# Attention on one core: prob x val in bursts of four key chunks, and the row maxima dealt anew over the units of a slot

## What is computed

```python
x = x + _L0_conv_ref(_gn(x), Wq, bq, Wk, bk, Wv, bv)     # layer 0
    q = q.reshape(B * NUM_HEADS, S, hd)                  # k and v alike; S = 1024, hd = 64
    scores = jnp.einsum('gqd,gkd->gqk', q, k) / sqrt(hd)
    attn = jax.nn.softmax(scores, axis=-1)
    wv = jnp.einsum('gqk,gkd->gqd', attn, v)             # "prob x val"
x = x + _L1_conv_ref(_gn(x), ...)                        # layer 1: masked relu, 3x3 convolution
```

## Time and profile before

| | us |
|---|---|
| median of 3 runs (2612.68 to 2613.2) | 2612.98 |
| the profiled execution | 2614.79 |
| its span in the trace | 2613.0 |
| PE busy in it | 2527.8 (97%) |
| DVE busy | 1942.0 (74%) |
| POOL busy | 1139.0 (44%) |
| ACT busy | 1089.0 (42%) |

### The profile page before, as it was taken

One profiled execution on the slowest core, in us unless ns is written; L12 is line 12 of the kernel. 1 busy time (PEld: TensorE's weight loads), 2 busy tenths in 40 slices (PEclk: granted clock), 3 DMA queues, 4 the chain that ended last, 5 costly groups with the idle time before them and its releaser, 6 DMA issues.

```text
span 2613.0 us, 39802 instructions
## 1 busy us (share of the span) xinstructions
PE 2527.8 (97%) x11848; PEld 994.2 (38%) x11848; DVE 1942.0 (74%) x2646; ACT 1089.0 (42%) x1803; POOL 1139.0 (44%) x971
## 2 busy tenths in 40 slices
PE   6999999999999999999999999988999999999998
PEld 2333333333333333333333333332344444444443
DVE  5877787787788787777778888886576967967415
ACT  4455455455545545545554554446232132132100
POOL 1465476566557646655664765545103012030000
PEclk9999999999999999999999999999999999999999
DMA  5324243251533415333242442511443734633533
GB/s 157 83 71 117 67 128 87 60 136 50 127 82 97 111 36 142 91 79 105 71 120 73 117 105 57 132 49 61 161 170 131 271 130 161 239 132 129 199 117 151
DMA packets 209638, 300.63 MB, mean 115 GB/s; under 512 B 82192, under 2 KB 131472, under 8 KB 209424
## 3 DMA queue, kind: packets, MB, share of 16 engines
q1 hardware_dynamic: 209424, 297.97, 38.3%
HBM read 194.49 MB, written 52.69 MB: 95 GB/s over the span
## 4 chain that ended last, share of the span: by engine, by line
PE 83%; DVE 9%; issue 3%; DMA 2%; ACT 1%; SPq 1%; POOL 1%; DVEq 0%; ACTq 0%; POOLq 0%
PE bank L844 27%; PE bank L747 15%; PE bank L721 14%; PE bank L676 11%; PE bank L694 7%; PE bank L686 6%; DVE nmax L1261 2%; DVE prob_sum L1255 2%; PE bank L710 1%; ACT prob L927 1%; PE bank L702 1%; PE bank L734 1%; DVE bn L221 1%; DVE qk_lo L1247 1%; SPq L414 1%
## 5 line engine op out<-in xcount | busy, mean ns | idle before, releaser
L1261 DVE TENSOR_REDUCE nmax<-bank 128x1 f32<-128x512 f32 x1024 | 658.2, 682 | 222.9 <-PE bank L694 215.6
L927 ACT ACTIVATE prob<-bank 128x512 f32<-128x512 f32 x1024 | 555.9, 595 | 589.3 <-PE bank L721 573.2
L844 PE MATMUL bank<-v,u_slab 128*128 128x512 f16 x3456 | 748.6, 380 | 0.0
L1090 POOL TENSOR_TENSOR prob_sum<-prob_sum,prob 128x512 f32<-128x512 f32 x354 | 513.3, 1450 | 371.7 <-ACT prob L927 370.6
L747 PE MATMUL bank<-prob,val 128*64 128x512 f32 x2048 | 497.5, 607 | 0.0
L844 PEld LDWEIGHTS bank<-v,u_slab 128*128 128x128 f16 x3456 | 338.5, 98 | 408.2 <-issue 3.0
L694 PE MATMUL bank<-k_a,q_a 128*128 128x512 f16 x1024 | 384.6, 382 | 18.3 <-DVE nmax L1261 12.3
L1255 DVE TENSOR_TENSOR prob_sum<-prob_sum,prob 128x512 f32<-128x512 f32 x354 | 356.5, 1007 | 11.4 <-DVE shift L1271 8.9
L721 PE MATMUL bank<-q_a,k_a 128*128 128x512 f16 x1024 | 315.2, 381 | 17.0 <-ACT prob L927 16.1
L721 PE MATMUL bank<-q_b,k_b 128*128 128x512 f16 x1024 | 305.2, 380 | 1.4 <-DMA q_b<-shift 1.1
L747 PEld LDWEIGHTS bank<-prob,val 128*64 128x64 f32 x2048 | 124.6, 136 | 238.3 <-issue 192.9
(11 more groups left out here) (139 smaller groups left out, 2503.6 us busy)
## 6 DMA issues: line engine op xcount, KB each, us to landing
u_slab<-u_scratch SPq DMA_DIRECT2D x72, 1024.0 KB, 5.0
xs<-x SPq DMA_DIRECT2D x28, 1024.0 KB, 5.5
tile<-x_scratch SPq DMA_DIRECT2D x26, 1024.0 KB, 6.2
u_scratch<-u_w SPq DMA_DIRECT2D x96, 192.0 KB, 2.7
q_a<-qk_hi SPq DMA_DIRECT2D x64, 256.0 KB, 4.8
den_sb<-recip_scratch SPq DMA_DIRECT2D x128, 128.0 KB, 2.9
x_scratch<-xr SPq DMA_DIRECT2D x16, 1024.0 KB, 4.4
xr<-x SPq DMA_DIRECT2D x15, 1024.0 KB, 7.6
```

Of the source, the lines that this page charges most:

```text
L844: mm = pe.matmul(bank_at(pos, co)[:].rearrange("p (i n) -> p i n", i=2), slab[:, l, c, co * P:(co + 1) * P], image[v][:, 2 * c:2 * c + 2, ...
L927: act.activation(prob[:, (2 * u + e) % 8], sc_bank[bank_turn(s * 16 + 2 * u + e, 16 * HPI)[0]][:], ACT.Exp, scale=float(D) ** -0.5).then_i ...
L1090: nc.gpsimd.tensor_tensor(acc, in0, prob[:, (2 * kc + 1) % 8], ALU.add).then_inc(s1["sum1"], 1)
L1261: dve.tensor_reduce(nmax[:, m // 2, m % 2:m % 2 + 1], src[:], AX.X, ALU.max, negate=True)\
```

## The change

In slots with projections (`has_projections`) the probabilities are multiplied in bursts of four key chunks: chunks 0 to 3 at the end of unit 4 and 4 to 7 at the end of unit 0 of the next slot; where s % 4 = 2 the second four stay in two pairs, 4,5 in unit 6 and 6,7 in the next unit 0. Other slots keep their four pairs. In the same slots the maxima are dealt 3, 3, 1, 3, 3, 3 over units 0 to 5. No instruction is added or removed; they stand in another order. Of `exp_tile` and its waits nothing is changed.

```diff
+MAX_QUOTA_FOURS = [3, 3, 1, 3, 3, 3, 0, 0]
...
-def ring_items(u, nxt, prev, v_units, stat):
+def ring_items(u, nxt, prev, v_units, stat, quota):
...
+def has_projections(s, more):
+
+    return s % HPH < 3 and (s < HPH or more)
...
+def max_quota(s, more):
+
+    return MAX_QUOTA_FOURS if has_projections(s, more) else MAX_QUOTA
...
+def pv_burst(s, u, more):
+
+    if not has_projections(s, more):
+        at = {2: (0, 1), 4: (2, 3), 6: (4, 5), UNITS: (6, 7)}
+    elif s % HPH == 2:
+        at = {4: (0, 1, 2, 3), 6: (4, 5), UNITS: (6, 7)}
+    else:
+        at = {4: (0, 1, 2, 3), UNITS: (4, 5, 6, 7)}
+    return at.get(u, ())
...
                     if u == 0 and prev:
-                        weigh_pair(h - 1, (s - 1) % HPI, SEG // 2 - 1, den_direct(s - 1, more))
-                    if u >= 2 and u % 2 == 0:
-                        weigh_pair(h, s, u // 2 - 1, den_direct(s, more))
+                        weigh_burst(h - 1, (s - 1) % HPI, pv_burst((s - 1) % HPI, UNITS, more), den_direct(s - 1, more))
+                    weigh_burst(h, s, pv_burst(s, u, more), den_direct(s, more))
```

More of the change, by code:

```diff
@@ L98, in bank_turn @@
     return bank_of(n), next(d for d in range(1, period) if bank_of(n - d) == bank_of(n))
-def ring_items(u, nxt, prev, v_units, stat):
-    first = sum(MAX_QUOTA[:u])
-    tiles = [("max", first + k) for k in range(MAX_QUOTA[u])] if nxt else []
+def ring_items(u, nxt, prev, v_units, stat, quota):
+    first = sum(quota[:u])
+    tiles = [("max", first + k) for k in range(quota[u])] if nxt else []
     at = {"a": tiles[0:1], "b": tiles[1:2], "c": tiles[2:]}
@@ L749, in weigh, with weigh_burst @@
                               stop=(kc == SEG - 1)).then_inc(s1["pv_done"], 1)
-            def weigh_pair(h, s, n, direct=False):
-                for kc in (2 * n, 2 * n + 1) if direct else ():
+            def weigh_burst(h, s, chunks, direct=False):
+                for kc in chunks if direct else ():
                     sum_prob(h, kc)
-                for kc in (2 * n, 2 * n + 1):
+                for kc in chunks:
                     weigh(h, s, kc)
@@ L764, in slot @@
                     items = ring_items(u, nxt, "direct" if den_direct(s - 1, more) else prev, proj and r == 2,
-                                       stat_units(s, more))
+                                       stat_units(s, more), max_quota(s, more))
                     def run(place):
@@ L828, in _ @@
                 slot(B - 1, s, nxt=s < HPI - 1, more=False)
-            weigh_pair(B * HPI - 1, HPI - 1, SEG // 2 - 1, True)
+            weigh_burst(B * HPI - 1, HPI - 1, pv_burst(HPI - 1, UNITS, False), True)
             def group_sum(pair, k):
```

## The result

| | before | after |
|---|---|---|
| median, us | 2612.83 (4 runs, 2611.42 to 2613.20) | 2626.91 (4 runs, 2624.99 to 2633.04) |
| profiled execution | 2614.79 | 2624.99 |
| its span | 2613.0 | 2623.2 |

The ratio is 1.0054, with a 95% interval of 1.0041 to 1.0067: the changed kernel is slower by half a per cent. Between the medians lie 14.1 us, between the spans of the two profiled executions 10.2. The forecast was 2622.3, and 2624.1 for the profiled execution, 9.3 us more than before.

A forecast was written before the change was run, and what follows sets the result against it. PE's own instruction order was taken to bound the slots. Bursts -11.3, ACT +12.9, DVE +5.5, slots 2 and 6 +0.7 and edges +1.5 made +9.3 on 2612.98: 2622.3 us, range 2609 to 2641 (own case 2618.5 to 2629).

The forecast's parts named there:

- Check (6): Profile sign: a full image of the loop grows by 1.2 us.
- The bursts, -11.3: Slots with projections: 75 bursts of probability matmuls fewer, each saving PE 0.15 us; -11.3 us.
- ACT, +12.9: Slots 0, 1, 4, 5: unit 6 too short for ACT, so unit 7's second matmul waits 0.51 us (slot 1: 0.24).
- Check (1): Profile sign: PE's wait for exponentials rises 8 to 10 us, some 22 idle times of 0.35 in unit 7.
- check 5: Profile sign: from unit 2 to unit 3 PE does not wait for ACT.
- DVE, +5.5: Slots 0 and 1: unit 2 too short for DVE with moments; unit 3's third maximum waits 0.42 us, 13 times.
- check 3: Profile sign: unit 3's third maximum waits for DVE by 0.4 us in slots 0 and 1, not 4 and 5.
- Slots 2 and 6, +0.7: New unit 3 waits of 1.05 us replace old ones of 1.0: net +0.05 in 14 slots.
- check (4): Profile sign, slots 2 and 6: unit 3's third maximum waits 0.5 us, the value projection 0.55.
- The rival of the port: Slots 2 and 6: POOL's adding starts before DVE's and takes the port; +18 us, 2640 us; 20%.
- Edges, +1.5: Very first slot about +1 us, last image between -1 and +2; +1.5 us taken for both, an estimate.
- The savings alone: Rival: PE stays unbroken and only the saved bursts show, 2601.7 us; 10%.

The follow-up runs named there:

- experiment 10: Kernel before, with only one burst of four in unit 4 of slots 4 and 5, replacing the pairs of units 2 and 4, old maxima; 2609.76 us, 0.9986.
- Experiment 3: Changed kernel, but slots 0, 1, 4 and 5 keep a pair of chunks 4,5 in unit 6, with 6,7 in the next unit 0; 2621.45 us, 1.0033.
- experiment 4: Changed kernel, but ACT evacuates unit 5's last projection behind the first exponential of unit 6, not ahead of it; 2632.79 us, 1.0074.
- Experiment 6: Changed kernel, but in unit 2 of slots 0 and 1 DVE copies the sums ahead of the two moments; 2623.47 us, 1.0034.
- experiment 2: Kernel before with only the maxima dealt 3,3,1,3,3,3 in slots with projections, all bursts as before; 2611.29 us, 0.9989.
- experiment 8: Kernel before with only the maxima of slots 2 and 6 dealt 3,3,2,3,3,2; 2617.58 us, 1.0016.
- Experiment 5: Changed kernel, but the very first slot has the old maxima and pairs of chunks in units 2 and 4; 2620.44 us, 1.0024.
- experiment 9: Changed kernel undone but for the burst of four in unit 4 of slots 4 and 5 and the new maxima, old first slot; 2607.58 us, 0.9980.
- experiment 7: Changed kernel with pair 4,5 in unit 6 of slots 0, 1, 4, 5; slots 2 and 6 rearranged; sums first; old first slot; 2613.33 us, 0.9998.
- experiment 1: Changed kernel's bursts with the maxima dealt as before, 2,3,3,3,3,2; 2652.42 us, 1.0155.

## Why the prediction was right, step by step

**The bound.** PE's order is the time in the slots; DVE's busy share fell to 72% instead of rising. Check (6), a full image, measured +1.4 for +1.2. The medians moved by 14.1 us for the 9.3 forecast, and the interval of the ratio, 10.7 to 17.5 us, leaves 9.3 just out; the spans of the profiled executions moved by 10.2.

**The bursts, -11.3.** Right. 3.59 us for four chunks (check 2), 0.15 a burst, and experiment 10 shows it alone.

**ACT, +12.9.** Right in mechanism, place and size: 0.52 for 0.51 in slots 0, 4, 5 and 0.28 for 0.24 in slot 1. Check (1) asked for some 22 equal idle times; 21 are there, of the 0.35 foretold, and the 22nd, slot 1 of the last image, has none. The sum of the list rose by 7.0 us and not by 8 to 10, since older waits for ACT went. Experiment 3 takes the waits away with a pair of chunks as cover, and in experiment 4 ACT's work has no room in the other order either. The case that the same order makes a wait from unit 2 to unit 3 was excluded by 0.17 us of slack, and none is there (check 5): unit 2 lasts 1.75 and unit 3 4.10 in slots 4 and 5.

**DVE, +5.5.** The mechanism is right (check 3: slots 0 and 1, not 4 and 5), and the size was 0.30 for 0.42: I had let the bank be freed 0.2 us behind the end of the copy, and it took 0.11. So 13 x 0.30 = 3.9. Experiment 6 removes it from unit 3. What I did not ask was who else takes a ring bank behind the moments: the statistics' matmul in unit 4 of slot 1, 7 x 0.49 = 3.4 us. So the two together cost 7.3 us for 5.5.

**Slots 2 and 6, +0.7.** Right by check (4), 0.42 and 0.64 for 0.5 and 0.55. The old waits went (in slot 6 where they were named, in slot 2 they stood in units 0 to 3, 1.03 us), and the new ones took their place; only unit 5 of slot 6 was missed, 7 x 0.32 = 2.2 us. The rival of the port came as close as was said, 0.05 us, and was decided for DVE in all slots. Experiments 2 and 8 put the wait elsewhere and kept it, which I had not expected of them.

**Edges, +1.5.** The weakest term. I had -1 to +2 for the last image and +1 for the first slot. Beyond the +1.4 of an ordinary image, image 0 lost 5.7 us, and the last image gained 5.5 us. I had seen the three maxima ahead of the first slot's shift, but priced them by one DVE instruction, and not by the addings ahead of the shift, which grew from 2.37 to 3.44 us, nor by the burst's cover gone from there, which together left PE 2.93 behind the shift's DMA. Experiment 5 gives up to 3.9 of it back. In the last image I took DVE to be late by itself, so that PE's savings would be lost. Five bursts less are 0.75 of the 5.5, and the two stretches of half clock less are up to 3.4, which no step of mine had. DVE's busy time fell there too, from 167.9 to 162.9 us; whether that made the image shorter is not shown, for experiment 6 has 162.4 and takes 204.4. The sum of both edges came out near zero, where I had +1.5, and neither part was right: that was luck.

**How the errors add up.** Against the forecast, the spans have +3.4 for the statistics' matmul and +2.2 for unit 5 of slot 6, and -1.6 for the size of the DVE term, -0.7 for slots 2 and 6, some -1.8 for the jumps and -0.6 for the edges; this leaves +0.9 us. The savings and the ACT term came as forecast (-11.3, and 21 x 0.52 + 7 x 0.28 = +12.9); that the rest came to so little is luck too.

**The median.** The profiled execution was 0.9 us off the forecast for it. The median lies 1.9 us above that execution and the forecast median 1.8 below its own, which makes the 4.6 us between 2622.3 and 2626.91: the four executions of the changed kernel spread over 8 us, and the 20 of the kernel before beside experiments 9 and 10 over 9, so that a median of four is no surer than a few us. Against the range of 2618.5 to 2629 of my own case that matters little.

**The rivals.** The savings alone (2601.7) did not come, and both waits appeared. The race for the port was won, by the margin forecast. Experiment 10 shows where the savings alone can be had, and experiment 9 has them too.

## What to carry to other kernels

Merging work that leaves one place and joins another has two prices: the switch saved, which is small and sure (0.15 us here), and the cover that the moved work gave to another engine at the place it leaves, which must be looked up there engine by engine. Merge only where the in-order chain of every other engine between the two neighbours is shorter than what stays (here unit 2 of slots 4 and 5: 2607.58 us), and leave the rest. And where an engine is short of time over a whole stretch, dealing its work anew moved the wait in all the deals tried here; the first pass of a pipeline, which lacks the cover of the others, may want an order of its own (experiment 5).

## What the runs showed of the hardware

**The jump of a hardware loop.** At the jump, in slot 0 to 1 of every image of the loop, PE and ACT have times without an instruction. PE in the kernel before, and ACT in the same place:

```profile
541.79 0.39 PE L694 MATMUL bank<-k_a,q_a 128*128 128x512 f16 x1 [0.89 <-issue]
...
544.14 1.09 ACT L927 ACTIVATE prob<-bank 128x512 f32<-128x512 f32 x2 [1.93 <-PE bank L721]
```

PE loses some 0.8 to 1.1 us there in each image before (unit 7 of slot 0 takes 4.45 to 4.74 us for 3.68). ACT lies idle 1.9 us. The scores are printed as the cause, but they end at 542.61, 1.5 us ahead of the exponential. What is late is ACT's own sequencer: the trace has its branch at 541.01 and the next instruction behind the branch, which waits for nothing, at 543.90. From the one to the other are 2.7 to 3.1 us at the five jumps before and 2.4 to 3.7 in the changed kernel and in the other experiments, but 4.4 to 4.9 in experiments 3 and 7, for the same instructions of ACT in the same order; with them come the 3.71 and 3.75 us with no cause. Why there are these two lengths is open: no run was made for it. The short one costs unit 1 of slot 1 nothing, behind a pair of chunks (before) as behind a burst of four (changed); the long one, which came only with a pair there, costs 1.0 to 1.8 us.

**DVE and POOL on one port.** DVE's busy time fell from 1942.0 to 1894.4 us though it has the same instructions. Half of it is the splitting of q and k, by line from both traces, before and after (busy and mean ns, then idle ahead):

```profile
L1247 DVE TENSOR_TENSOR qk_lo<-qk,qk_hi 128x512 f16<-128x512 f32 x128 | 128.2, 1002 | 24.7 <-ACT qk_hi L918 9.5 <-DVE den_sb L1287 8.3 <-DVE shift L1271 5.3
```

```profile
L1268 DVE TENSOR_TENSOR qk_lo<-qk,qk_hi 128x512 f16<-128x512 f32 x128 | 103.4, 808 | 24.7 <-ACT qk_hi L939 9.5 <-DVE den_sb L1308 8.3 <-DVE shift L1292 5.3
```

The 354 addings give another 14.5 us (342.0 for 356.5). These instructions of two operands in SBUF seem to fall less often into one of POOL's; that is my reading of their shorter means, and no run takes POOL away to show it. It comes with the bursts, not with the deal: DVE is busy 1905.4 us with the bursts alone (experiment 1) and 1946.7 with the maxima alone (experiment 2). At 479.18 DVE was ahead by 0.05 us and kept its 0.68 us while POOL's adding took 1.76; with POOL ahead it was DVE that took 1.16. The Trainium skill ("SBUF — State Buffer", SBUF: two separate sides) says that the first of the two to start holds the pair of ports for its whole instruction. The trace agrees in both directions: whoever came second took longer by 0.48 and 0.49 us than its 0.68 and 1.27 alone, 0.13 and 0.14 less than the rest of the other's record. In the two slots with POOL's record 0.01 and 0.02 us ahead DVE held the ports all the same: that close, the start in the record does not tell who is first.
